# Mixture-of-experts block of a gated cross-attention layer: where the next unit's up weights are split in the last step of a unit

## The reference

```
x = x + tanh(g_xattn) * attention(layernorm(x), ctx)          # 16 heads of 32, causal
t = layernorm(x)
route = sigmoid(t @ router_w); e = argmax(route)              # one of 8 experts for each token
h = silu(t @ gate_w[e]) * (t @ up_w[e])                       # 512 -> 1024
x = x + tanh(g_ffn) * max(route) * (h @ down_w[e])            # 1024 -> 512
```

## Time and profile before

| | us |
|---|---|
| median of 3 runs | 538.55 |
| lowest and highest of them | 537.9, 545.1 |
| the profiled execution, its own time | 541.25 |
| span that its profile covers | 539.6 |

### The profile page before, as it was taken

How to read it: one execution, slowest core, us unless ns; L and a number is a source line. 1 busy time by engine, 2 the same in 40 slices (tenths; PEclk the granted TensorE clock), 3 DMA queues, 4 the chain that set the end, 5 groups by cost and what they waited for, 6 DMA issues and landing times.

```text
span 539.6 us, 11376 instructions
## 1 busy us (share of the span) xinstructions
PE 473.4 (88%) x3659; PEld 399.4 (74%) x3659; DVE 384.1 (71%) x809; ACT 308.5 (57%) x871; POOL 167.7 (31%) x210
## 2 busy tenths in 40 slices
PE   0988999899999999754799989989999998999990
PEld 0976796688679767553788878878788797888870
DVE  3674877967886487875377778777787777778751
ACT  0566747764876577220556556565565665666630
POOL 3325315534552644235212122231222212220121
PEclk9995999999999999955899999999999999999996
DMA  8600210440130034644365786768767778677620
GB/s 189 192 3 2 83 27 1 132 131 2 49 118 15 1 94 121 208 123 90 109 205 160 248 246 187 228 196 256 236 200 229 214 243 250 191 235 226 193 67 30
DMA packets 58911, 77.32 MB, mean 143 GB/s; under 512 B 5074, under 2 KB 40506, under 8 KB 58880
## 3 DMA queue, kind: packets, MB, share of 16 engines
q1 hardware_dynamic: 53728, 66.90, 41.8%
q0 software_dynamic: 5152, 10.03, 6.3%
HBM read 67.76 MB, written 10.34 MB: 145 GB/s over the span
## 4 chain that ended last, share of the span: by engine, by line
PE 47%; DVE 18%; DMA 11%; issue 10%; ACT 7%; POOL 2%; SPq 1%; ACTq 0%; DVEq 0%; POOLq 0%
DMA staging<-in_L_ffn_up_w 8%; PE gate_banks L1791 6%; PE bank L1405 5%; PE bank L1407 4%; PE bank L1406 4%; PE bank L1512 3%; PE up_banks L1791 3%; DVE gu_lo L891 3%; ACT gu_hi L664 3%; PE gate_banks L1793 3%; DMA staging<-in_L_xattn_Wq 2%; DVE xn L1381 2%; PE gate_banks L1499 2%; PE bank L1523 2%; DVE x_hl L891 2%
## 5 line engine op out<-in xcount | busy, mean ns | idle before, releaser
L1791 PE MATMUL gate_banks<-x_hl,gu_hi 128*128 128x448 f32 x256 | 87.0, 390 | 12.6 <-DVE x_hl L891 8.6
L891 DVE TENSOR_TENSOR gu_lo<-staging,gu_hi 128x1024 fp32r<-128x1024 f32 x64 | 78.3, 1223 | 19.4 <-ACT gu_hi L664 19.1
L1791 PE MATMUL up_banks<-x_hl,gu_hi 128*128 128x448 f32 x256 | 82.9, 376 | 0.0
L493 POOL TENSOR_TENSOR pn<-pr,inv 100x400 f32<-100x400 f32 x64 | 54.4, 853 | 61.0 <-DVE inv L1062 60.8
L664 ACT ACTIVATE gu_hi<-staging 128x1024 fp32r<-128x1024 f32 x64 | 67.0, 1051 | 5.5 <-DMA staging<-in_L_ffn_gate_w 3.9
L1793 PE MATMUL gate_banks<-x_hl,gu_lo 128*128 128x224 f32 x256 | 69.4, 271 | 0.0
L1793 PE MATMUL up_banks<-x_hl,gu_lo 128*128 128x224 f32 x256 | 68.1, 266 | 0.0
L1791 PEld LDWEIGHTS gate_banks<-x_hl,gu_hi 128*128 128x128 f32 x256 | 49.7, 194 | 21.2 <-issue 13.4
L664 ACT ACTIVATE wkv_hi<-qT 128x448 fp32r<-128x448 f32 x32 | 18.5, 578 | 71.4 <-DVE qT L1366 71.4
L715 ACT ACTIVATE pr<-gate_banks,nmx 100x100 f32<-100x100 f32 x128 | 42.2, 355 | 17.7 <-DVE nmx L1056 17.5
L1791 PEld LDWEIGHTS up_banks<-x_hl,gu_hi 128*128 128x128 f32 x256 | 48.1, 188 | 4.3
(11 more groups left out here) (229 smaller groups left out, 1114.9 us busy)
## 6 DMA issues: line engine op xcount, KB each, us to landing
staging<-in_L_ffn_gate_w SPq DMA_DIRECT2D x32, 512.0 KB, 5.8
staging<-in_L_ffn_up_w SPq DMA_DIRECT2D x32, 512.0 KB, 7.4
staging<-in_L_ffn_down_w SPq DMA_DIRECT2D x32, 512.0 KB, 4.5
x_rows<-x SPq DMA_DIRECT2D x8, 800.0 KB
xt<-in_x SPq DMA_DIRECT2D x4, 800.0 KB
xr<-in_x SPq DMA_DIRECT2D x16, 200.0 KB
staging<-in_L_xattn_Wq SPq DMA_DIRECT2D x1, 1024.0 KB, 11.0
x<-in_L_xattn_Wout SPq DMA_DIRECT2D x1, 1024.0 KB, 9.4
```

What stands on the lines that cost most here:

```text
L493: nc.gpsimd.tensor_tensor(pn[0:S, n % DEEP], pr[0:S, n % 2], inv[0:S, n % HP].unsqueeze(2).to_broadcast([S, HP, S]), ALU.mult).then_inc(pr ...
L891: return nc.vector.tensor_tensor(dst, src, hi.bitcast(F32), ALU.subtract)
L1791: nc.tensor.matmul(pair[:, m, 0:2 * CAP], gu_hi[:, s, w, k, r], x_hl[:, :, k, 0:CAP], start=k == 0, stop=False, skip_group_check=True)
```

## The change

In step 3 of a unit, and only there (`tokens` is true), the split of the next unit's up weights moves. On ScalarE it stood behind the silu and ahead of the tokens; now it stands behind the tokens and the copy for the up sum. On VectorE it stood between the low gate weights and the tokens; now it stands behind the tokens and the up sum, ahead of the product with the silu. Nothing is added or removed, and the other three steps are as before. TensorE's, GpSimd's and SP's programs don't change.

```
@@ ScalarE, step @@
                 nc.scalar.activation(silu_g, gate_sum, ACT.Silu).then_inc(silu_done.sem, 1)
-                if after:
+                if after and not tokens:
                     split(*after, 1)
                 act.wait_ge(gu_ready.sem, gu_ready.after(u, j + 1))
                 if tokens:
                     split_tokens(u + 1)
                 act.wait_ge(up_sum_done.sem, up_sum_done.after(u, j))
                 copy(up_low, up_rest).then_inc(up_low_done.sem, 1)
+                if tokens:
+                    split(*after, 1)
                 act.wait_ge(h_done.sem, h_done.after(u, j + 1))
@@ VectorE, step @@
                 if after:
                     split(*after, 0)
-                    split(*after, 1)
+                    if not tokens:
+                        split(*after, 1)
                 if tokens:
                     split_tokens(u + 1)
                 dve.wait_ge(up_low_done.sem, up_low_done.after(u, j + 1))
                 nc.vector.tensor_tensor(up_sum, up_low, up_main, ALU.add).then_inc(up_sum_done.sem, 1)
+                if tokens:
+                    split(*after, 1)
                 dve.wait_ge(up_sum_done.sem, up_sum_done.after(u, j + 1))
```

## The result

Over 20 runs each, the changed kernel has a median of 536.31 us and the kernel before 539.1 us. The medians lie 2.8 us apart. The ratio, taken over all the runs, is 0.9938, 95% interval 0.9911 to 0.9965, so the change gains 3.3 us (1.9 to 4.8). The forecast was a gain of 5.5 us. The profiled execution took 538.37 us, its span is 536.7 us in place of 539.6.

A forecast was written before the change was run, and what follows sets the result against it. The VectorE-ScalarE handover chain, beneath PE's hole, was taken to set the gain: six boundaries gain 5.6 us, boundary 0 loses 0.1, so 541.25 - 5.5 = 535.75 profiled, 533.0 on the runs' median. Range 529.5 to 538.0.

The forecast's parts named there:

- the rival of the late loads: At the boundaries, gate and up loads slip 0.7 us each against the chain, leaving a gain of 1.5 us; chance 0.15.
- The hand-over chain of VectorE and ScalarE: At boundary 1, handovers without idle time, 7.50 us from high up weights to next gate sum, set the gain, 1.03 us.
- TensorE's hole: PE waits for low tokens at each boundary, 1.55 us at boundary 1; rival that it decides: gain 8.4 us, chance 0.14.
- Tokens earlier, hole gone: At boundary 1, tokens start 1.45 us after high gate weights, ready 0.55 us before PE is free; the 1.55 us hole closes.
- Up weights later but covered: At boundary 1, low up weights are done at 322.51 and PE asks for them near 323.9: covered by 1.4 us.
- The chain from high up weights to gate sum: At boundary 1, high up weights to the next gate sum shrinks from 7.50 to 5.61 us; gain 1.03 us.
- all boundaries: Boundaries 1 to 6 gain between 0.84 and 1.04 us each, together 5.6; boundary 0 loses 0.1; sum 5.5 us.
- What is late next: One unit on, in step 1, PE's 0.43 us slack is used up: waits of 0.1 to 0.4 us for `wq_lo`.
- Against the new place: ScalarE and VectorE run first in, first out; low up weights now precede the product, so a late up load stops it.
- Signs of being wrong: PE waiting for `gu_lo` at the up half, a gate load wait over 1.5 us, or granted clock under 1.00 in units.

The follow-up runs named there:

- early loads: SP issues the next unit's gate and up loads ahead of step 3's down load: 4.1 us faster than before with the old order, 4.5 with the change's.
- The second profile: The change, unaltered, profiled once more beside a second profile of the kernel before: step 3 sums 61.90 and 66.14 us, a gain of 4.2 us.

## Why the prediction was right, and where it was off

- **The time itself says little.** 536.31 us lies in the range, but nearer to the rival of the late loads (537.1) than to the forecast (533.0), and the range took in both. Half a microsecond of the distance is the kernel before, whose median is 539.1 over 20 runs and was 538.55 over 3; the rest is gain that did not come. The interval of the gain, 1.9 to 4.8, leaves out the 5.5 us of the forecast. What shows the mechanism is the rows, not the number. (The price of the loads rival also leaves out the 0.1 us that boundary 0 loses.)
- **What bounds the kernel: right.** The hand-over chain of VectorE and ScalarE sets the time, not TensorE's hole. With only VectorE's order changed the hole shrank by two thirds, the chain grew by 0.1 us per boundary, and the time didn't fall.
- **Tokens earlier, hole gone: right.** At boundary 1 the tokens start 1.44 us behind the high gate weights (1.45 forecast), and TensorE doesn't wait for them at any boundary.
- **Up weights later but covered: right.** TensorE never waited for `gu_lo` halfway through the first product.
- **The chain from high up weights to gate sum: right.** 7.50 to 5.61 us was forecast; 5.62 was measured at boundary 1, and 7.51 where VectorE's order was left and the clock was full.
- **The sum over the boundaries: too large by about 2 us.** The step that failed is *all boundaries*: "6 terms between 0.84 and 1.04". It took the start of the tokens as bound by the high gate weights everywhere but at boundary 0. They have a second bound, TensorE's release of their buffer. With early loads and the new order it stands alone, here at boundary 1 (TensorE's last up matmul, then the gate sums at both ends of step 3):

```profile
319.01 0.27 PE L1806 MATMUL up_banks<-x_hl,gu_lo 128*128 128x224 f32 x1
```

```profile
317.53 0.61 DVE L1364 TENSOR_TENSOR v<-v,gate_banks 128x448 f32<-128x448 f32 x1
...
326.29 0.61 DVE L1364 TENSOR_TENSOR v<-v,gate_banks 128x448 f32<-128x448 f32 x1
```

  The release, at 319.01 + 0.27 = 319.28, comes 1.75 us behind the gate sum, and the next gate sum 7.01 us behind the release. The shortest step 3 of the new order at boundaries 1 to 6 is therefore some 8.74 us, in four profiles. At boundary 3 the forecast amounted to 9.27 - 0.84 = 8.43, and at boundary 6 to 8.96 - 0.85 = 8.11. Both lie below that floor, by 0.31 and 0.63 us, together 0.9 us. I used the floor at boundary 0 and didn't ask about it at the others.
- **The rest, about 1.2 us, was nearly all the loads** of that execution: the rival "the loads take it back" in small. It is 1.0 us over the floor at boundaries 3, 4 and 6 and 0.1 at boundary 1. At boundaries 3, 4 and 6 the high gate weights start 8.10, 8.14 and 7.92 us behind the down load's issue, where before it was 7.38, 7.69 and 7.08. The second profile has 4.2 us of gain, so this part comes and goes. The 3.3 us of the 20 runs lies near the lower of the two. Boundary 0 lost 0.16 us in place of 0.1, since the tokens started 0.12 us behind the release and not 0.05.
- **What is late next: right in kind, wrong in place.** TensorE's lead is lost again, but in step 0, to `finish` (3.4 us), and not to `wq_lo` in step 1. I compared TensorE's slack with the low down weights of step 1 and overlooked that the down product of step 0 also waits for the rows of the unit before. The trace of the kernel before had it, with only 0.14 us to spare (334.37 + 1.40 = 335.77 against 335.91), so that losing 0.5 us had to give a wait of about 0.4; it was 0.43:

```profile
334.37 1.40 DVE L1381 SCALAR_TENSOR_TENSOR xn<-bank,x 112x512 f32<-112x512 f32 x2
```

```profile
335.91 0.40 PE L1405 MATMUL bank<-wq_hi,wkv_hi 128*112 128x512 f32 x1
```

  It is also what closes the loop: `finish` releases TensorE's down product, TensorE's work up to the release of the tokens' buffer follows, then tokens, up copy, up split, product, and again `finish`. With early loads this loop takes 326.29 - 293.58 = 32.71 us per unit, with no wait for a load at a boundary; its two hand-overs stand in that profile as waits, seven times each: TensorE for `finish` (2.4 us in all) and ScalarE for the release (4.5 us).
- **Against the new place:** that a late up load would now stop the product as well was not tested, since no up load was late. The opposite case was: with early loads the new place costs 0.15 us per boundary.
- **Signs of being wrong:** none appeared. TensorE didn't wait for `gu_lo` at the up half, the longest wait for a gate load was 1.0 us, and the granted clock was 1.00 in the units.

What stays open is why the same three loads, issued in the same spacing, land up to 0.9 us apart from boundary to boundary. The gather of residual rows, the one suspect named here, is neither shown nor ruled out: a run would have to make GpSimd wait for the high up weights of the unit after.

## What to carry to other kernels

When an engine with 95% busy time waits a little at one place, look at what its neighbours do without a pause: removing the wait gains only what the chain behind it gains. Laying two orders side by side gives the new length of a step; then go through every wait of the moved instruction, since the second latest takes over as soon as the latest goes. Ahead of moving a split behind a late load, ask whether the load can be early: here moving the load gained about as much as moving the split, and moving the silu behind the up split in every step gained 5.5 us against 3.3, though the intervals of these two overlap. And look in the trace whether the edit of an experiment moved what it was to move, before reading its time.

## What the hardware showed that was not expected

- The part ahead of the gate sum of unit 0's step 3 took between 283.0 and 289.4 us in nine profiled executions of kernels that compute the same instructions in the same order up to there. That is twice what the change gains. The two profiles of the change differ by 3.6 us in their spans, but behind that point by only 0.9 us. So most of the scatter of the run times, which leaves 1.5 us either side after 20 runs, probably lies ahead of the units.
- Outside step 3, and in the kernels that leave the silu ahead of the up split, VectorE's steps repeat nearly to a hundredth of a microsecond over executions and kernels (8.87, 7.54 and 7.55 us) as long as neither a load nor TensorE holds them up. Where TensorE lagged, with only ScalarE's order changed, single steps took 7.71 and 8.38 us. Comparing step times in two profiles told kernels apart that the run times could not (60.43 against 61.48 us in sum).
- With the loads issued in one fixed spacing (the gate load 1.60 to 1.65 us behind the down load), the high gate weights started between 6.96 and 8.14 us behind the down load's issue. The low end is not a load time: at 6.96 ScalarE did not wait for the load. Where it did wait, the load landed 7.27 to 8.14 us behind.
- TensorE's granted clock fell to 0.50 for some 2 to 3 us in three of seven places where it had stood 2.27 to 2.49 us, and stayed at 1.00 in four others with the same stand (2.27 to 2.52 us). Its gate product then took up to 4.18 us in place of 2.60.
